# Softmax sums of the first four routed rows from the row scores by ScalarE, the others summed in groups of up to three blocks

## The reference, cut to what matters

```python
gating = softmax(x @ W_gate.T); idx = argmax(gating); indicator = one_hot(idx, H)
q, k, v = split(x @ W_qkv.T, 3)                       # k, v: (B, T, H, hd), hd = 32
k_shared = einsum('bth,bthd->btd', indicator, k)
v_shared = einsum('bth,bthd->btd', indicator * top1_val, v)
att = einsum('bhqd,bkd->bhqk', q, k_shared) / sqrt(hd)
att = softmax(where(causal, att, -inf))
y = einsum('bhqk,bkd->bhqd', att, v_shared)
```

## Time and profile before

| | us |
|---|---|
| median of 3 runs (lowest, highest) | 720.44 (716.49, 721.85) |
| the profiled execution | 713.84 |
| its span, first to last instruction | 712.6 |
| mean granted clock of TensorE in it | 0.976 of full speed |

### The profile page before, as it was taken

How to read it: one execution, slowest core, us unless ns; L and a number is a source line. 1 busy time by engine, 2 the same in 40 slices (tenths; PEclk the granted TensorE clock), 3 DMA queues, 4 the chain that set the end, 5 groups by cost and what they waited for, 6 DMA issues and landing times.

```text
span 712.6 us, 19601 instructions
## 1 busy us (share of the span) xinstructions
PE 656.5 (92%) x7497; PEld 528.4 (74%) x7497; DVE 515.7 (72%) x1361; ACT 364.9 (51%) x907; POOL 426.0 (60%) x350
## 2 busy tenths in 40 slices
PE   3797999899997999979988789999999999999996
PEld 3575888778886888868877567777777777777775
DVE  3976686478774786657775789888788787978554
ACT  4453544434544346433545046465555566556674
POOL 2972856185761758536673047476867787777740
PEclk9999999999999999999999788999999999999999
DMA  8523112131222221311216610141314041403011
GB/s 295 186 58 89 46 56 97 51 93 62 66 79 64 64 73 51 102 47 55 65 41 168 184 46 25 41 112 28 105 48 106 25 128 31 123 26 84 4 33 32
DMA packets 64015, 55.06 MB, mean 77 GB/s; under 512 B 6320, under 2 KB 48688, under 8 KB 63920
## 3 DMA queue, kind: packets, MB, share of 16 engines
q1 hardware_dynamic: 61760, 52.87, 25.4%
q10 hardware_dynamic: 2160, 0.93, 0.5%
HBM read 35.63 MB, written 17.89 MB: 75 GB/s over the span
## 4 chain that ended last, share of the span: by engine, by line
PE 45%; DVE 3%; issue 1%; POOL 1%; ACT 1%; DMA 0%; DVEq 0%; POOLq 0%; ACTq 0%
PE s_ps L1015 13%; PE st_ps L1046 11%; PE od_ps L1060 10%; PE od_ps L1074 5%; PE gemm L897 2%; PE s_ps L1083 1%; PE gemm L983 1%; PE s_ps L1085 1%; DVE qkv L1216 1%; POOL p_loc L1606 1%; DVE s_ps L1290 1%; ACT p_loc L1457 1%; PE win L957 1%; DVE l_sum L1240 0%; DMA w_tok<-w_tok 0%
## 5 line engine op out<-in xcount | busy, mean ns | idle before, releaser
L897 PE MATMUL gemm<-w_tok,xt 128*128 128x512 f32 (+1 forms) x768 | 179.6, 381 | 2.9 <-DVE qt L1223 1.4
L1290 DVE CUSTOM_DVE_ANT_0 s_ps<-s_ps,x_ln 128x512 f32<-128x512 f32 (+3 forms) x240 | 138.3, 626 | 31.3 <-PE s_ps L1015 30.3
L897 PEld LDWEIGHTS gemm<-w_tok,xt 128*128 128x128 f32 x768 | 132.7, 194 | 28.4 <-DVE qt L1223 2.1
L1015 PE MATMUL s_ps<-k_stack,w_tok 96*128 96x512 f32 (+2 forms) x368 | 115.6, 398 | 2.2 <-DVE w_tok L1301 1.7
L1046 PE MATMUL st_ps<-w_tok,k_stack 98*128 98x512 f32 x288 | 103.4, 423 | 1.0 <-DMA w_tok<-w_tok 0.8
L1504 ACT ACTIVATE p_loc<-st_ps 128x512 f32<-128x512 f32 x144 | 77.9, 599 | 45.0 <-PE st_ps L1046 42.9
L1015 PEld LDWEIGHTS s_ps<-k_stack,w_tok 96*128 96x128 f32 x368 | 64.8, 199 | 28.7 <-issue 11.5
L1290 DVE CUSTOM_DVE_ANT_0 s_ps<-s_ps,x_ln,picked_fk 128x128 f32<-128x128 f32 (+3 forms) x128 | 64.9, 554 | 8.4 <-PE s_ps L1015 7.7
L1457 ACT ACTIVATE p_loc<-win,l_max 128x96 f32<-128x96 f32 x256 | 61.1, 392 | 12.3 <-DVE l_max L1231 12.2
L1582 POOL TENSOR_TENSOR rope_b<-qkv,sin_t 128x128 f32<-128x128 f32 (+1 forms) x32 | 27.4, 879 | 65.1 <-DVE qkv L1198 65.0
L1566 POOL TENSOR_TENSOR rms_y<-rms_v,minus_half 128x20 f32<-128x20 f32 x16 | 58.6, 3663 | 9.3 <-DVE rms_v L1208 9.3
(11 more groups left out here) (171 smaller groups left out, 1283.3 us busy)
## 6 DMA issues: line engine op xcount, KB each, us to landing
w_tok<-q_parts SPq DMA_DIRECT2D x96, 128.0 KB, 2.7
q_parts<-qt SPq DMA_DIRECT2D x128, 64.0 KB
x_ln<-x SPq DMA_DIRECT2D x8, 512.0 KB, 4.9
x_res<-x SPq DMA_DIRECT2D x16, 256.0 KB, 3.5
partial<-x_res SPq DMA_DIRECT2D x16, 256.0 KB, 2.2
k_t<-partial SPq DMA_DIRECT2D x8, 512.0 KB, 5.7
raw<-w_tok SPq DMA_DIRECT2D x3, 1024.0 KB, 13.5
v_win<-v_rows SPq DMA_DIRECT2D x64, 48.0 KB, 2.2
```

What stands on the lines that cost most here:

```text
L897: i = e.matmul(g[:, 0:cols], xs[l][:, k, a * P:(a + 1) * P], w_tok_p[r][:, k, c0:c0 + cols], start=first, stop=last)
L1015: e.matmul(s_ps[bank][:, 0:cols], q_op[b][0:HALVES, i, h, :], k_stack[0:HALVES, b * S + c0:b * S + c0 + cols], start=True, stop=True).then ...
L1290: e.tensor_tensor_reduce(out=s[:, 0:cols], in0=s[:, 0:cols], in1=causal[:, S - width + c0:S - width + c0 + cols], scale=1.0, scalar=dst if ...
```

## The change

For rows 0 to 3 of each unit (IN_ROWS = 4) the sums of weights no longer come from the key scores. After VectorE has written the masked and scaled row scores back to their bank and their extreme to r_max, ScalarE takes the exponential of the bank, with r_max as its bias, in place, and adds it up over the columns (accum_out) into `r_sum`. For that the maxima are now the minima of the scores times -ROUTED_SCALE. The bank of s_ps (or gemm[1] and tp1 in the first maxima) comes free with rs_sum (first_sum) in place of rs_max. These rows have no key_sums, their row_done copies only the values, and one reciprocal of 16 columns, in the finish of row 0, does for all four.

In rows 4 to 7 up to three blocks are added before a key_sums: groups of 3 and 2, of 3 and 3, of 3, 2 and 2, and of 3, 3 and 2 blocks. A third block is added to p_sum in place. The sums are turned back by a whole transpose, and the reciprocal reads every 32nd column. The planner knows of the exponentials (0.2 us + 0.00078 us a column on ScalarE).

```diff
+IN_ROWS = IT // 2
+
+SUM_OF, OPENS_SUM, ENDS_SUM = {}, set(), []
+for _i in range(IN_ROWS, IT):
+    _k, _count = _i * (_i + 1) // 2, -(-(_i + 1) // 3)
+    for _n in range(_count):
+        _size = (_i + 1 - _n + _count - 1) // _count
+        for _m in range(_k + 1, _k + _size):
+            SUM_OF[_m] = len(ENDS_SUM)
+        if _size > 1:
+            OPENS_SUM.add(_k + 1)
+            ENDS_SUM.append(_k + _size - 1)
+        _k += _size
...
+def exps(cols):
+
+    return 0.2 + cols * 0.00078
...
-        bank = self.take_s(("row_scores", u, t), ("rs_max", (u, t)))
+        bank = self.take_s(("row_scores", u, t), ("rs_sum" if i < IN_ROWS else "rs_max", (u, t)))
...
+        if i < IN_ROWS:
+            self.s_free[bank] = self.busy(end + 0.1, ("A", exps(cols))) + HOP
...
-            for m in row_sums(i):
+            for m in row_sums(i) if i >= IN_ROWS else ():
...
-                e.transpose(turned_back(u, i)[:, 0, :], o_sb[i % 2][:, 0, :], idt[:, :])
-
-                mm = e.matmul(turned_back(u, i)[:, 1, 0:HQ], o_sb[i % 2][:, 1, :], idt[:, 0:P:DK], start=True, stop=True)
+                mm = e.transpose(turned_back(u, i)[:, 0, :], o_sb[i % 2][:, 0, :], idt[:, :])
+                if i >= IN_ROWS:
+                    mm = e.transpose(turned_back(u, i)[:, 1, :], o_sb[i % 2][:, 1, :], idt[:, :])
...
-                    scale=1.0, scalar=dst if c0 else NEG, op0=ALU.add, op1=ALU.max, accum_out=dst).then_inc(
+                    scale=-ROUTED_SCALE, scalar=dst if c0 else -NEG, op0=ALU.add, op1=ALU.min, accum_out=dst).then_inc(
                         *M["rs_max"].did((u, t)))
...
+                if i == 0:
+                    lane.wait_ge(*sums_of_rows(u))
+                    e.reciprocal(r_rec[:, :, :], r_sum[u % 2][:, :, :]).then_inc(*M["ro_rec"].did((u, i)))
+                elif i >= IN_ROWS:
+                    e.reciprocal(rec, turned_back(u, i)[:, 1, 0:P:DK]).then_inc(*M["ro_rec"].did((u, i)))
...
+            elif step == "row_scores":
+                u, hg, b, t = key
+                i, h, c0 = MAXIMA[t]
+                if i < IN_ROWS:
+                    s, cols = s_ps[plan.turn["s", ("row_scores", u, t)]], (i + 1) * P
+                    lane.wait_ge(*M["rs_max"].of((u, t)))
+                    if u >= 2:
+                        lane.wait_ge(*M["ro_rec"].of((u - 2, 0)))
+                    e.activation(s[:, 0:cols], s[:, 0:cols], ACT.Exp, bias=r_max[:, i, h:h + 1], scale=-1.0,
+                                 accum_out=r_sum[u % 2][:, i, h:h + 1]).then_inc(*M["rs_sum"].did((u, t)))
...
-                e.activation(o_sb[i % 2][:, :, :], od_ps[:, 0:2, :], ACT.Copy).then_inc(*M["ro_r"].did((u, i)))
+                parts = 1 if i < IN_ROWS else 2
+                e.activation(o_sb[i % 2][:, 0:parts, :], od_ps[:, 0:parts, :], ACT.Copy).then_inc(
+                    *M["ro_r"].did((u, i)))
```

More of the change, by code:

```diff
@@ L409, in first_maxima @@
                     room = (("gemm", 1), "tp1")[t % 2]
-                    p.take(room, ("first_max", t), ("first_max", t))
+                    p.take(room, ("first_max", t), ("first_sum" if i < IN_ROWS else "first_max", t))
                     cols = min(width - c0, 512)
@@ L415, in first_maxima @@
                         yield None
-                    p.busy(p.now, ("V", 0.4 + cols / 960))
+                    p.busy(p.now, ("V", 0.4 + cols / 960), *[("A", exps(cols))] * (i < IN_ROWS))
                     t += 1
@@ L536, in next_scores @@
             whats.append(self.done["values", before])
-            whats.append(self.done.get(("pair", before), self.done.get(("sum", before))))
-        if k in PAIR_OF:
-            n = u * len(PAIR_OF) + PAIR_OF[k] - SUMS
+            if PRODUCTS[before % len(PRODUCTS)][0] >= IN_ROWS:
+                whats.append(self.done.get(("pair", before), self.done.get(("sum", before))))
+        if k in OPENS_SUM:
+            n = u * len(ENDS_SUM) + SUM_OF[k] - SUMS
             if n >= 0:
@@ L597, in take_values @@
             self.do("row_done", u, b, i)
-            self.values_free = self.copied[u * IT + i] = self.busy(self.now + 0.1, ("A", 0.38)) + HOP
+            self.values_free = self.copied[u * IT + i] = self.busy(self.now + 0.1, ("A", 0.27 if i < IN_ROWS else 0.38)) + HOP
         self.valued += g + 1 - k
@@ L801, in mixed_attention_kernel @@
     o_rec = small.piece(HQ)
+    r_sum = [small.piece(IN_ROWS, HQ) for _ in range(2)]
+    r_rec = small.piece(IN_ROWS, HQ)
     res = [k_t[:, b, HALF:HALF + S].rearrange("p (i c) -> p i c", i=IT) for b in range(B)]
@@ L1482, in scalar_program @@
                     lane.wait_ge(*M["r_row"].of((u - 1, int(u == 1))))
-                e.activation(hi.bitcast(F32R), max_rows(u, part), ACT.Copy, scale=-1.0).then_inc(*M["r_t"].did((u, part)))
+                e.activation(hi.bitcast(F32R), max_rows(u, part), ACT.Copy,
+                             scale=1.0 / ROUTED_SCALE).then_inc(*M["r_t"].did((u, part)))
                 lane.wait_ge(*M["r_t"].of((u, part)))
@@ L1508, in scalar_program @@
                 u, b, i = key
-                lane.wait_ge(*M["rsum"].of((u, row_end(i))))
+                if i < IN_ROWS:
+                    lane.wait_ge(*M["rpv"].of((u, row_end(i))))
+                else:
+                    lane.wait_ge(*M["rsum"].of((u, row_end(i))))
                 if i >= 2:
```

102 lines of the change are left out of this document (63 added, 39 removed).

## The result

The change makes the kernel slower: 724.97 us median (723.80 to 727.47, eight runs) against 718.35 (714.10 to 721.85, eight runs) of the kernel before, a ratio of 1.0100 with a 95% interval of 1.0066 to 1.0134. Forecast were 712.0 us, with 699 to 732 as the range: the time is inside it, the sign is wrong. The profiled execution of before was one of its short ones (span 712.6 us), that of after a usual one (span 725.2 us).

The account below looks back on a forecast made before the run. TensorE was taken to bound the routed stage, with ScalarE taking over in rows 0 to 3. Seven intervals -7.7, end -2.7 and start +2.0 gave -8.4 us: 712.0 us from 720.44, range 699 to 732.

Parts of the forecast that it names:

- What leaves TensorE, 2.7 us a unit, 21.6 in all: Routed stage: ten groups of key_sums (2.2 us) and four turned sums (0.5) leave TensorE in each of eight units.
- GpSimd and VectorE, nothing: Routed units: GpSimd stays at 28.2 us a unit with 16 additions; VectorE's maxima take the same 0.65 us at 512 columns.
- ScalarE's time, 8.6 us a unit: Each routed unit: 16 new exponentials with accumulator readings on ScalarE, 8.6 us, ends 8.4 and 10.3.
- The first part, 12.2 us: Unit's stretch with maxima of rows 0 to 3: ScalarE bounds it, 8 key scores instead of 11, 1.5 us longer.
- my 1.7: End of the maxima of rows 0 to 3: VectorE goes on to row 4 1.7 us before ScalarE is through.
- The rival with nothing moved: Stretch of rows 0 to 3 keeps 11 key scores, VectorE gets no lead: 15.3 us there, 734.4 us in all; chance 0.15.
- The second part, 22.2 us: Unit's stretch with maxima of rows 4 to 7: TensorE sets its length, 22.2 us against 24.8 before.
- the seven intervals: Between transposes of the maxima, 424.2 to 670.0 us: 1.1 us gained for a unit, 7.7 in all.
- The start, +2.0: First 16 maxima, through two banks beside the first stage's last rounds: 2.0 us lost, 3.3 at most.
- The tail, -2.7: From 670 us on, without row scores of a next unit: TensorE sets the pace and the whole 2.7 us are gained.
- The rival that ScalarE takes all of it, 719.7 us: Routed units: the stretch of rows 0 to 3 grows as much as that of rows 4 to 7 shrinks; chance 0.26.
- The clock rival, 726 us: TensorE, waiting for ScalarE in rows 0 to 3, falls to 1.2 GHz for some 5 us: 2 us a unit; chance 0.10.

Follow-up runs that it names:

- run without exponentials: Changed kernel with all its new exponentials left out and a constant for the sums of rows 0 to 3: 700.38 us, ratio 0.974 to the kernel before.
- rows mixed: Changed kernel with the row maxima of units 1 to 7 in the order 0, 4, 1, 5, 2, 6, 3, 7: 723.12 us, 1.0081.
- run with free banks: Changed kernel without unit 0's new exponentials; those of units 1 to 7 use SBUF, so banks come free after VectorE's maximum: 719.34 us, 1.0026.
- eight columns: Changed kernel without unit 0's new exponentials; those of units 1 to 7 read 8 columns of their bank, all waits kept: 705.63 us, 0.9818.

## Why the prediction was wrong, step by step

- **What leaves TensorE, 2.7 us a unit, 21.6 in all.** Right in kind, too large in a middle unit. The run without exponentials is 18.7 us faster than before (16.7 by the medians): 1.8 us a unit between the transposes (35.8 to 34.1) and 6.4 at the end (42.6 to 36.3).
- **GpSimd and VectorE, nothing.** Right. GpSimd is busy 426.2 us against 426.0, no wait for its sums is among TensorE's longest, and at 32.7 of 35.1 us a unit it still does not bound. VectorE's maxima last 626 and 555 ns on average over the run against 626 and 554 before.
- **ScalarE's time, 8.6 us a unit.** Right: 8.2. A reading of the accumulator lasts 227 ns in its row, but the next activation starts 0.09 us into it.
- **The first part, 12.2 us.** Here the forecast failed. Its step "with fewer key scores ready in time I put 8 instead of 11 there" is wrong at both ends: before's first part had 13 exponentials of key scores, not 11, and eleven stand among the sums between 577.8 and 591.1 us. So two moved away, where I had three move from a smaller number. Three more than my 8, by 0.49 us, are 1.5 us; 14 sums in place of 16 and a lead other than my 1.7 took back a part, and the first part is 13.3 us, 1.1 more than forecast. The rival with nothing moved had eleven too, but by the same misreading, and 15.3 us there: VectorE does get a lead.
- **The second part, 22.2 us.** It is 22.9. I gave it to TensorE alone, but two sums lie in it and ScalarE has no pause until 596.5 us, 5.4 us into it; TensorE's waits for the sums' banks go on there (1.0 us). With both parts this unit is 36.3 us in place of 34.4. Over the six units it is 36.5 us each in place of 35.8 - 1.1 = 34.7, 11 us in all. For the seven intervals I had forecast -7.7 and the profiles show +9.0 (4.7 and 4.3 in the table), 16.7 apart; the 5.8 that the six units leave are unit 1, which had 30.8 us before and has 35.5.
- **The start, +2.0.** It was +8.1 in the profile, of which 0.9 stood before the first maxima, in a part that the change does not touch. The other 7.1 are above my bound of 3.3, and so are the 4 to 6 us of the two other profiles with these exponentials. The bound was for the maxima alone; the late banks also carry the last output projections, TensorE waits for ScalarE (2.07 us at 409.29), and from 388.0 to 409.3 us its granted clock is 0.76 on average, where before it was 1.00 from 384.0 to 401.2. What all that is worth at the end is another matter: without the first exponentials the time fell only by 2 us, within the noise.
- **The tail, -2.7.** -4.4: here nothing is in the way. With it the misses add up to the 21.0 us between the forecast -8.4 and the spans' +12.6: 6.1 at the start, -0.1 in unit 0, 16.7 in the seven intervals, -1.7 here. The short profile of before is a part of them; by the medians the forecast of 712.0 us was 13.0 us too low.
- **The rival that ScalarE takes all of it, 719.7 us.** Nearest in mechanism: the first part grew by 2.6 us and the second shrank by 1.9. It had put the two equal.
- **The clock rival, 726 us.** Nearest in number, and mostly wrong in its place: the clock is 1.00 in both parts of the unit above and in four of the six. What it describes did happen once, in the 38.2 us unit: ScalarE is busy without a break from 542 to 554 us, TensorE has only 10 records of matmuls from 546.0 to 549.9, and the granted clock is 0.50 from 549.9 to 553.3 us. That unit is 1.7 to 1.9 us longer than those at 1.00; I had given the rival 2 us in every unit. It is lower in unit 1 too (0.81 from 432.2 to 467.7 us, 0.89 in before's unit 1) and a part of the 4.7 us lost there. Without exponentials it is 0.84 in that unit, and the unit takes 31.2 us, so the clock alone does not make the loss.

ScalarE's time for the sums was foreseen; how much of it comes out at TensorE was not. Wrong was the belief that an engine with 36.2 - 28.8 = 7 us of idle time in each unit hands on only what overflows in one stretch. In after's unit the idle time does lie in gaps of the second part, before key scores that are not there yet, and the sums stand in the first. But that they stand there is not the cause: with the rows mixed the sums were spread over the unit, ScalarE had as much idle time as in after's unit (28.6 of 36.1 us busy), and no more of its idle time was used. What the runs show is that ScalarE's time costs, and that of each further row a larger share comes out again at TensorE. Why the idle time can't be used wherever the sums stand stays open. That each sum and each key score waits in one queue behind the other kind, with few banks between the engines, would fit the waits; no run here changed the number of banks.

## What to carry to other kernels

Work taken off the bounding engine and given to one that is 60% busy in that stage is not free because the busy time still fits. Here the first row paid, of the others a third to over two thirds of ScalarE's time came back, and spreading the sums over the stage changed nothing beyond the noise. Count the queue in the stretch where the work arrives, with all that stands there by the trace, and do not count on much of it moving away. The price of a unit of work rises with the load already there, so give it in small portions and measure each: here one row of four was a gain of 1.6% and four rows a loss of 1%. To tell "the engine's time costs" from "the hand-over costs", take two runs: keep every wait and cut the instruction's length, and keep the length and cut the wait.

## What the runs showed of the hardware

An exponential over SBUF was not cheaper for ScalarE than one in place in PSUM: 0.40 and 0.71 us from start to start at 128 and 512 columns (597.77 to 598.17, 607.56 to 608.27, in the run with free banks) against 0.36 and 0.66 in the change. Their records read 394, 510, 618 and 731 ns for 128, 256, 384 and 512 columns, and 343, 465, 612 and 766 in the change. An activation's mean duration also depends on what stands beside it: the key scores' exponentials read 636 ns on average in the change and 602 with eight columns (groups above L1536's in the same answers), while three in a row still take 1.57 us in both when ScalarE was idle before them. Such a mean is no measure of a slower instruction; the distance of starts is.
